# Attention probabilities turned by a product with a diagonal of reciprocal row sums, in a two-layer kernel on one core

## Chip, cores and metric

The kernel runs on one core of one Trainium2 chip. The metric is the device time of one execution in microseconds (us), as the median of several runs. TensorE (PE) does the matrix products, VectorE (DVE), ScalarE (ACT) and GpSimd (POOL) the elementwise work, SyncE (SP) issues the transfers. PEld is the loading of a product's stationary operand, which can run beside a product.

## What is computed

A normalised input goes through causal latent attention and through a routed mixture of 32 experts, and both results are added to the input. Cut to what matters here, for 2 sequences of 1024 tokens and 16 heads:

```python
scores = jnp.einsum('bthd,bshd->bhts', q, k) * scale
scores = jnp.where(causal[None, None], scores, jnp.finfo(scores.dtype).min)
probs = jax.nn.softmax(scores, axis=-1)
out = jnp.einsum('bhts,bshd->bthd', probs, v).reshape(b, t, H * D)
return out @ wo
```

The softmax divides each row of exponentials by its sum. The kernel works with the exponentials and divides later.

## The kernel before

Three stages follow one another. `prepare` normalises the input and makes latents; `attend` does the attention (from about 50 to 731 us of the profiled span); `mix` does the experts.

**Tiling of the attention.** Heads go in 8 pairs (`e` is the head within a pair), each for 2 sequences (`b`), so there are 16 pair steps, numbered `s`. A pair step goes through 8 query tiles `t` of 128 queries. The first tile sees 128 keys, the last 1024. Each engine runs an order written out by hand: `body(i)` lists, per engine, what it does in tile `t` for heads 0 and 1, and semaphores tie the engines together.

**One tile of one head.** PE makes the scores in `ps_s` by `scores` (lines 662 to 664). DVE adds the mask, takes the row maximum and leaves it in `nm` by `maximum` (line 1032). ACT takes exponentials into `prob` and row sums into `lsum` by `exponent` (line 859). PE turns `prob` block by block (128 queries by 128 keys) into `ps_t` by `turn` (line 675), one tile later than the scores. ACT and DVE copy `ps_t` to `pt` by `take_turned` (lines 869 and 1041). PE multiplies the turned blocks with the values by `values` (line 690), two tiles later than the scores, into `ps_o`; the two heads use one half of `ps_o`'s partitions each. A tile `t` has `t + 1` blocks per head, so a pair step has 2 x 36 blocks and the stage has 1152.

**The division.** `ps_o` holds outputs with queries along the free axis, so the reciprocals have to lie along that axis too. After four tiles (a half, `c`) DVE takes the 8 reciprocals per partition by `invert` (line 1048). ACT widens them to 512 columns by `widen` (line 876). PE turns these by `spread` (line 708, the entries `L0` and `Lp` of the hand-written order), ACT takes the result to `rec` (line 882), and DVE multiplies `ps_o` by it into `on` by `normalise` (line 1054). `on` is split into a high and a low part (`out_hi` on ACT, `out_low` on POOL) and goes through `out_products` (lines 719 to 721); DVE adds the result to `yacc` (line 1061).

**Beside this** the order places the projections for the next pair step: PE makes them (line 638), DVE and POOL rotate them (`rope_products` on DVE, lines 997 and 998; lines 1193 and 1195 on POOL), and DVE splits weights in `split_a` (lines 1013 to 1019).

**Kinds of product.** `turn` and `spread` call `nc.tensor.transpose` on float32, with the data as stationary operand and the unit matrix `ident` as moving one. `values` (line 690), the gate and key products in `prepare` (lines 317 and 324), and the folding of weights (line 63) are float32 products by `nc.tensor.matmul`. Line 324 has 8 products for each of 4 chunks, with a stationary operand of 128 columns and 96 moving columns; line 63 has 4 per call, 128 stationary and 64 moving columns; line 317 has 6 per chunk with 512 moving columns. The scores and projections use the float32r format.

Of the kernel before, what the change touches and what calls it, by code (L numbers as in the profile page):

```python
# [33 lines left out]
P = 128  # L34
# [364 lines left out]
STAGE = ["QR0", "Lp", "KR0", "QL0", "QR1", "KR1", "Yp0", "Yp1", "L0", "B", "QL1", "WA", "Y0", "Y1"]  # L399
TURNS = {"QR0": "W0", "KR0": "W1", "QL0": "W2", "QR1": "W3"}  # L400
SPARE = {"Lp": 0, "QR1": 0, "W3": 0, "KR0": 1, "KR1": 1, "W1": 1}


def misc_order(first=False, last=False):
# [3 lines left out]
    for b in range(B):  # L408
        for name in STAGE:
            if (name in ("B", "WA") and b) or (first and b == 0 and name in ("Lp", "Yp0", "Yp1")):  # L410
                continue
# [75 lines left out]
def attend(nc, d, keep):  # L487
    ctx = ExitStack()
    with ctx:
# [11 lines left out]
        rec, on, ohi, olo = tensors(nc, ctx, [  # L501
            ("rec", [P, CH], F32), ("on", [P, CH], F32), ("ohi", [P, CH], F32R), ("olo", [P, CH], F32R)])
# [4 lines left out]
        nm, lsum, linv = tensors(nc, ctx, [("nm", [P, 2], F32), ("lsum", [P, 2, TPC, 2], F32), ("linv", [P, 2, TPC, 2], F32)])  # L507
# [8 lines left out]
        def bank_of(b, name):  # L516

            if b is None:
# [12 lines left out]
        linv_done, widened, rec_copied, on_done, ohi_done, olo_done, y_added = (sem("linv_done"), sem("widened"), sem("rec_copied"), sem("on_done"),  # L531
                                                                       sem("ohi_done"), sem("olo_done"), sem("y_added"))
# [14 lines left out]
        def consumed(i, b, name):  # L547
# [11 lines left out]
            if name in ("L0", "Lp"):  # L559
                return rec_copied, s * 2 + (name == "L0")  # L560
# [35 lines left out]
        def _(pe):  # L596
# [71 lines left out]
            def turn(s, t, e, g):  # L668
# [42 lines left out]
            def reciprocals(i, b, name, s, c):  # L711
                pe.wait_ge(widened, s * 2 + c + 1)
                side(i, b, name, spread)
# [15 lines left out]
            def body(i):  # L729
                for b in range(B):  # L730
# [4 lines left out]
                    def also(name):  # L735
# [10 lines left out]
                        elif name == "Lp":  # L746
                            if earlier:
                                reciprocals(i, b, name, s - 1, 1)
# [10 lines left out]
                    for t in range(TILES):  # L759
# [45 lines left out]
                        else:  # L805
# [4 lines left out]
                            if t < TILES - 1:  # L810
                                also(("L0", "QL1")[t - TPC - 1])
# [763 lines left out]
```

## Time and profile before

| | us |
|---|---|
| median of 3 runs | 1140.23 (1138.33 to 1140.56) |
| the profiled execution | 1139.54 |
| its span, first to last instruction | 1137.8 |
| PE busy in the span | 1109.4 (98%) |
| DVE busy | 733.0 (64%) |
| ACT busy | 635.4 (56%) |
| POOL busy | 487.4 (43%) |
| granted TensorE clock, mean | 0.998 |

The page of the profile lists groups of instructions by line: how many, their summed busy time and the mean of one. PE records overlap: a record shows when a product is in the array, and the next may start before its end. What a product costs is therefore read from the distance between starts in the view in order of time, not from its own duration. A float32 `matmul` of the program appears as two records, each with its own load of the stationary operand.

### The profile page before, as it was taken

To read this page: it belongs to the slowest core of one execution; us is meant where nothing else is said; L and a number is where in the kernel's file an instruction comes from. 1 tells how busy PE (TensorE), PEld (TensorE's weight loads), DVE (VectorE), ACT (ScalarE), POOL (GpSimd) and SP (SyncE) were. 2 spreads that over 40 slices of the span, in tenths; PEclk is the share of its full clock that TensorE was granted. 3 is DMA by queue.
4 is the path that set the end of the run, shared out by engine and by line. 5 is a ranking of instruction groups with operands and counts; after the bars stand their busy time and mean duration, and the time that the engine had idled before them with its cause. 6 is when DMAs were issued, how large, how long until landed. Compare 5 with 4: busy or idle time off the path is not lost. (4 is left out here: it accounts for less than half of the span.)

```text
span 1137.8 us, 23926 instructions
## 1 busy us (share of the span) xinstructions
PE 1109.4 (98%) x8096; PEld 948.7 (83%) x8096; DVE 733.0 (64%) x1540; ACT 635.4 (56%) x1285; POOL 487.4 (43%) x383
## 2 busy tenths in 40 slices
PE   6989999999999999999999999999999999999998
PEld 3668888888888888888888888788888888888887
DVE  6878778678688688687687775564444454444444
ACT  3575766766766766767667767443333333333332
POOL 0265455456456466456456452132333223333232
PEclk9999999999999999999999999999999999999999
DMA  8100000000000000000000021163333334333333
GB/s 295 56 19 19 3 19 20 1 18 18 0 17 19 0 18 18 0 17 19 0 18 0 1 66 31 43 190 115 111 111 115 97 119 145 111 115 97 117 109 101
DMA packets 26343, 67.87 MB, mean 60 GB/s; under 512 B 3061, under 2 KB 9461, under 8 KB 26297
## 3 DMA queue, kind: packets, MB, share of 16 engines
q1 hardware_dynamic: 26152, 67.24, 19.2%
q8 instruction: 23, 0.38, 0.1%
q14 instruction: 24, 0.19, 0.1%
q10 hardware_dynamic: 144, 0.07, 0.0%
HBM read 62.82 MB, written 4.47 MB: 59 GB/s over the span
## 5 line engine op out<-in xcount | busy, mean ns | idle before, releaser
L859 ACT ACTIVATE prob<-ps_s,nm 128x128 f32<-128x128 f32 (+7 forms) x256 | 189.7, 741 | 164.0 <-DVE nm L1032 162.1
L1468 POOL TENSOR_TENSOR qhi<-t,qhi 128x512 fp32r<-128x512 f32 x95 | 122.3, 1288 | 277.7 <-ACT qhi L1406 277.7
L1032 DVE CUSTOM_DVE_ANT_0 ps_s<-ps_s,causal 128x128 f32<-128x128 f32 (+7 forms) x256 | 195.4, 763 | 53.5 <-PE ps_s L664 45.8
L675 PE MATMUL ps_t<-ident,prob 128*128 128x128 f32 x1152 | 177.5, 275 | 3.5 <-ACT pt L869 2.3
L675 PEld LDWEIGHTS ps_t<-ident,prob 128*128 128x128 f32 x1152 | 136.5, 140 | 29.4 <-issue 9.9
L690 PE MATMUL ps_o<-pt,kvn 128*64 128x128 f32 x2304 | 154.0, 278 | 0.1
L690 PEld LDWEIGHTS ps_o<-pt,kvn 128*64 128x64 f32 x2304 | 123.2, 136 | 29.6 <-issue 16.5
L1440 DVE TENSOR_TENSOR t<-t,routing 128x512 f32<-128x512 f32 x64 | 45.0, 703 | 145.2 <-ACT t L1400 140.1
L1041 DVE COPY pt<-ps_t 128x128 f32<-128x128 f32 (+2 forms) x192 | 102.0, 531 | 49.2 <-PE ps_t L675 47.2
L1406 ACT ACTIVATE qhi<-t 128x512 fp32r<-128x512 f32 x95 | 60.1, 633 | 121.0 <-DVE t L1445 121.0
L1400 ACT ACTIVATE t<-ps_s 128x512 f32<-128x512 f32 x94 | 56.2, 598 | 124.6 <-PE ps_s L379 124.6
L869 ACT ACTIVATE pt<-ps_t 128x128 f32<-128x128 f32 (+2 forms) x192 | 97.0, 505 | 27.3 <-PE ps_t L675 24.7
L1214 POOL TENSOR_TENSOR olo<-on,ohi 128x512 fp32r<-128x512 f32 x31 | 39.9, 1287 | 141.9 <-ACT ohi L903 141.9
L1208 POOL TENSOR_TENSOR qlo<-t,qhi 64x512 fp32r<-64x512 f32 x62 | 79.2, 1278 | 48.1 <-ACT qhi L897 39.9
L1193 POOL TENSOR_TENSOR xtf<-xtf,sinv 128x512 f32<-128x512 f32 x62 | 80.0, 1291 | 17.9 <-DVE xtf L998 14.0
L1195 POOL TENSOR_TENSOR t<-t,xtf 128x512 f32<-128x512 f32 x62 | 79.8, 1286 | 4.9
L662 PE MATMUL ps_s<-keys,qhi 128*128 128x384 f32 (+4 forms) x192 | 75.7, 395 | 3.2 <-ACT prob L859 3.2
L662 PE MATMUL ps_s<-khi,qhi 128*128 128x384 f32 (+4 forms) x192 | 74.2, 386 | 0.1
L1335 PE MATMUL ps_y<-keys,qhi 128*128 128x256 f32 x256 | 72.3, 282 | 1.5 <-POOL qhi L1468 1.5
L1337 PE MATMUL ps_y<-keys,qhi 128*128 128x256 f32 x256 | 72.5, 283 | 0.0
L1336 PE MATMUL ps_y<-keys,qhi 128*128 128x256 f32 x256 | 72.4, 283 | 0.0
L1445 DVE TENSOR_TENSOR t<-t,ps_s 128x512 f32<-128x512 f32 x95 | 65.3, 687 | 9.3
(270 smaller groups left out, 2805.3 us busy)
## 6 DMA issues: line engine op xcount, KB each, us to landing
routing<-wT_scratch SPq DMA_DIRECT2D x34, 256.0 KB, 3.7
raw_a<-in_e SPq DMA_DIRECT2D x17, 384.0 KB, 3.0
cosv<-in_e SPq DMA_DIRECT2D x17, 384.0 KB, 3.0
sinv<-wT_scratch SPq DMA_DIRECT2D x17, 384.0 KB, 3.6
raw<-in_e SPq DMA_DIRECT2D x17, 384.0 KB, 3.1
routing<-wT_scratch SPq DMA_DIRECT2D x16, 384.0 KB, 3.3
raw_a<-in_a SPq DMA_DIRECT2D x8, 512.0 KB, 3.3
raw_b<-in_b SPq DMA_DIRECT2D x8, 480.0 KB, 4.0
```

Source lines behind the costliest of these rows:

```text
L662: nc.tensor.matmul(out[:, 0:width], qhi[b][e][:, q], khi[b][e][:, kk], start=True, stop=False, skip_group_check=True)
L675: mm = nc.tensor.transpose(ps_t[x][:, at * P:(at + 1) * P], prob[t % 2][e][:, j * P:(j + 1) * P], ident[:, :])
L690: mm = nc.tensor.matmul(ps_o[64 * e:64 * e + 64, at], kvn[:, b * 8 + j, :], pt[t % 2][:, e, j, :], start=j == 0, stop=j == t)
L859: nc.scalar.activation(prob[t % 2][e][:, 0:len(halves) * width].rearrange("p (h k) -> p h k", k=width), ps_s[e][:, 0:len(halves), 0:width] ...
L869: nc.scalar.activation(pt[t % 2][:, e, blocks[0]:blocks[-1] + 1, :].rearrange("p j q -> p (j q)"), ps_t[0][:, 0:len(blocks) * P], ACT.Copy ...
L1032: nc.vector.tensor_tensor_reduce(out=s_ps, in0=s_ps, in1=bias, scale=-1.0, scalar=-MASKED, op0=ALU.add, op1=ALU.min, accum_out=nm[:, e:e + ...
L1041: nc.vector.tensor_copy(pt[t % 2][:, e, blocks[0]:blocks[-1] + 1, :].rearrange("p j q -> p (j q)"), ps_t[1][:, 0:len(blocks) * P]).then_in ...
L1193: nc.gpsimd.tensor_tensor(sh[:, g, :], sh[:, g, :], sinv[:, c * CH:(c + 1) * CH], ALU.mult).then_inc(rope_sin, 1)
L1195: nc.gpsimd.tensor_tensor(t1[:, g, :], t1[:, g, :], sh[:, g, :], ALU.add).then_inc(rope_sum, 1)
L1208: nc.gpsimd.tensor_tensor(lo[to_b][e][rows, cs], t1[rows, g, :], hi[to_b][e][rows, cs].bitcast(F32), ALU.subtract).then_inc(rope_lo, 1)
L1337: mm = nc.tensor.matmul(to, hl[:, c, tokens], whi[q][:, wide], start=False, stop=True, skip_group_check=True)
L1468: nc.gpsimd.tensor_tensor(hl[:, c, :], hf[:, c, :], hh[:, c, :].bitcast(F32), ALU.subtract).then_inc(h_lo, 1)
```

## The change

The turn becomes a product that also divides. For each head and tile, DVE takes the reciprocals of the 128 row sums (`divide`: a reciprocal of one column, then `ident` times that column into `over`, a 128 x 128 diagonal matrix). `turn` waits for `over` and calls `nc.tensor.matmul` with `prob` as stationary operand and `over` as moving one, instead of `nc.tensor.transpose` with `ident`. The turned block then holds normalised probabilities. `invert`, `widen`, `spread` with `L0` and `Lp`, `take_reciprocals` and `normalise` go; ACT copies `ps_o` to `on` by `take_values` where it took `rec`. `add_out` of `Yp1` moves to a later place in tile 5 of DVE's order.

```diff
-STAGE = ["QR0", "Lp", "KR0", "QL0", "QR1", "KR1", "Yp0", "Yp1", "L0", "B", "QL1", "WA", "Y0", "Y1"]
+STAGE = ["QR0", "KR0", "QL0", "QR1", "KR1", "Yp0", "Yp1", "B", "QL1", "WA", "Y0", "Y1"]
...
-        nm, lsum, linv = tensors(nc, ctx, [("nm", [P, 2], F32), ("lsum", [P, 2, TPC, 2], F32), ("linv", [P, 2, TPC, 2], F32)])
+        nm, lsum, linv = tensors(nc, ctx, [("nm", [P, 2], F32), ("lsum", [P, 2, TPC, 2], F32), ("linv", [P, 2], F32)])
+        over = [[ctx.enter_context(nc.sbuf_tensor(f"over{par}{e}", [P, P], F32)) for e in range(2)] for par in range(2)]
...
-                pe.wait_ge(exp_done, s * U + 2 * t + e + 1)
+                pe.wait_ge(over_done, s * U + 2 * t + e + 1)
                 ge(pe, copied[x], before)
                 for at, j in enumerate(groups_of(t)[g]):
-                    mm = nc.tensor.transpose(ps_t[x][:, at * P:(at + 1) * P], prob[t % 2][e][:, j * P:(j + 1) * P], ident[:, :])
+                    mm = nc.tensor.matmul(ps_t[x][:, at * P:(at + 1) * P], prob[t % 2][e][:, j * P:(j + 1) * P], over[t % 2][e][:, :],
+                                          start=True, stop=True)
...
-            def spread(out):
-
-                for t in range(TPC):
-                    mm = nc.tensor.transpose(out[:, t * P:(t + 1) * P], rec[:, t * P:(t + 1) * P], ident[:, :])
-                return mm
...
-            def widen(s, c):
-
-                act.wait_ge(linv_done, s * 2 + c + 1)
...
-            def take_reciprocals(n, ps):
...
+            def take_values(s, c):
+
+                act.wait_ge(pv_done, 2 * (s * TILES + (c + 1) * TPC))
+                ge(act, olo_done, s * 2 + c)
+                nc.scalar.activation(on[:, :], ps_o[:, :], ACT.Copy).then_inc(on_done, 1)
...
-            def invert(s, c):
...
-            def normalise(s, c):
-                dve.wait_ge(rec_copied, s * 2 + c + 1)
-                dve.wait_ge(pv_done, 2 * (s * TILES + (c + 1) * TPC))
-                ge(dve, olo_done, s * 2 + c)
-                nc.vector.tensor_tensor(on[:, :], ps_o[:, :], rec[:, :], ALU.mult).then_inc(on_done, 1)
+            def divide(s, t, e):
+
+                dve.wait_ge(exp_done, s * U + 2 * t + e + 1)
+                nc.vector.reciprocal(linv[:, e:e + 1], lsum[:, t // TPC, t % TPC, e:e + 1]).then_inc(linv_done, 1)
+                dve.wait_ge(linv_done, s * U + 2 * t + e + 1)
+                nc.vector.tensor_scalar(out=over[t % 2][e][:, :], in0=ident[:, :], scalar1=linv[:, e:e + 1], scalar2=None,
+                                        op0=ALU.mult).then_inc(over_done, 1)
...
+                        if t == TPC:
+                            divide(s, t - 1, 1)
                         maximum(s, t, 0)
+                        if has and t != TPC:
+                            divide(sp, tp, 1)
...
+                            if t == TPC - 1:
+                                divide(s, t, 0)
                             if t > TPC:
                                 take_turned(sp, tp, 1, 1)
                             else:
                                 take_turned(sp, tp, 1, 0)
+                            if t != TPC - 1:
+                                divide(s, t, 0)
                             maximum(s, t, 1)
```

On PE, in tile 1 of a pair step with `b` = 1, this stood in a row before (`ps_o<-pt,kvn` are the values products, `ps_t<-ident,prob` the turns, `ps_s<-ident,rec` the turn of the reciprocals; the moving operand's name comes first):

```order
L662 MATMUL ps_s<-khi,qhi 128x256
L663 MATMUL ps_s<-klo,qhi 128x256
L664 MATMUL ps_s<-khi,qlo 128x256
L690 MATMUL ps_o<-pt,kvn 64x128 x16
L708 MATMUL ps_s<-ident,rec 128x128 x4
L675 MATMUL ps_t<-ident,prob 128x128 x2
L662 MATMUL ps_s<-khi,qhi 128x256
```

And this stands there after the change:

```order
L661 MATMUL ps_s<-khi,qhi 128x256
L662 MATMUL ps_s<-klo,qhi 128x256
L663 MATMUL ps_s<-khi,qlo 128x256
L690 MATMUL ps_o<-pt,kvn 64x128 x16
L674 MATMUL ps_t<-over,prob 128x128 x2
L661 MATMUL ps_s<-khi,qhi 128x256
```

The four turns of the reciprocals are gone, the turns of `prob` have `over` in place of `ident`, and nothing else moved.

On DVE, from the rotation at the start of tile 1 to the maximum of tile 2 (`ISA ps_s,nm<-ps_s,causal` is the maximum, `ISA nm` its read-out, `COPY pt<-ps_t` is `take_turned`, `on<-ps_o,rec` is `normalise`), before:

```order
L997 TENSOR_TENSOR t<-ps_x,cosv 128x512
L998 STREAM_SHUFFLE xtf<-ps_x 128x512
L1032 ISA ps_s,nm<-ps_s,causal 128x256
L1032 ISA nm 128x1
L1041 COPY pt<-ps_t 128x128
L1032 ISA ps_s,nm<-ps_s,causal 128x256
L1032 ISA nm 128x1
L1054 TENSOR_TENSOR on<-ps_o,rec 128x512
L1032 ISA ps_s,nm<-ps_s,causal 128x384
```

And after:

```order
L969 STREAM_SHUFFLE xtf<-ps_x 128x512
L1003 ISA ps_s,nm<-ps_s,causal 128x256
L1003 ISA nm 128x1
L1018 RECIPROCAL linv<-lsum 128x1
L1020 TENSOR_SCALAR over<-ident,linv 128x128
L1012 COPY pt<-ps_t 128x128
L1018 RECIPROCAL linv<-lsum 128x1
L1020 TENSOR_SCALAR over<-ident,linv 128x128
L1003 ISA ps_s,nm<-ps_s,causal 128x256
L1003 ISA nm 128x1
L1003 ISA ps_s,nm<-ps_s,causal 128x384
```

Each tile has two pairs of `RECIPROCAL` and `TENSOR_SCALAR` more, between the maxima; the product of `ps_o` with `rec` has left DVE.

## Rows read from the trace of the kernel before

**Rows 1.** The page, parts 1 and 2: busy time, and PE in 40 slices.

```profile
PE 1109.4 (98%) x8096; PEld 948.7 (83%) x8096; DVE 733.0 (64%) x1540; ACT 635.4 (56%) x1285; POOL 487.4 (43%) x383
...
PE   6989999999999999999999999999999999999998
```

**Rows 2.** Busy time of each engine in a stretch: the attention, 60 to 725 us.

```profile
core 0: us, PE busy (x) PEld busy (x) DVE busy (x) ACT busy (x) POOL busy (x), PEclk, DMA share, GB/s
...
60.00:725.00 665.00, 659.24 (x5563) 562.68 (x5561) 501.23 (x1156) 451.09 (x985) 355.92 (x277) 1.00 0.05 15
```

**Rows 3.** Instructions by line and shape: PE's float32 products; count, busy us, mean ns.

```profile
L675 PE MATMUL ps_t<-ident,prob 128*128 128x128 f32 x1152 | 177.5, 275 | 3.5 <-ACT pt L869 2.3 <-DVE pt L1041 1.2
L690 PE MATMUL ps_o<-pt,kvn 128*64 128x128 f32 x2304 | 154.0, 278 | 0.1
...
L708 PE MATMUL ps_x<-ident,rec 128*128 128x128 f32 x68 | 10.2, 273 | 0.0
...
L708 PE MATMUL ps_s<-ident,rec 128*128 128x128 f32 x60 | 9.8, 287 | 0.0
```

**Rows 4.** PE in order of time, one pair step: start us, length us, instruction, records.

```profile
307.91 1.06 PE L675 MATMUL ps_t<-ident,prob 128*128 128x128 f32 x8
308.73 0.48 PE L638 MATMUL ps_x<-q1hi,rhi 128*128 128x512 f32 x1
309.05 0.40 PE L638 MATMUL ps_x<-q1lo,rhi 128*128 128x512 f32 x1
309.28 0.40 PE L638 MATMUL ps_x<-q,rhi 128*128 128x512 f32 x1
...
310.42 1.97 PE L690 MATMUL ps_o<-pt,kvn 128*64 128x128 f32 x32
312.32 0.66 PE L708 MATMUL ps_s<-ident,rec 128*128 128x128 f32 x4
...
324.36 0.66 PE L675 MATMUL ps_t<-ident,prob 128*128 128x128 f32 x4
```

**Rows 5.** PE in order of time, in the first stage: float32 products, 128-column stationary operands.

```profile
28.02 1.92 PE L324 MATMUL ps_n<-wkg,xT 128*128 128x96 f32 x16
29.79 1.03 PE L63 MATMUL ps_t<-raw_a 128*128 128x64 f32 x8
30.65 5.37 PE L317 MATMUL ps_l<-xT,wl 128*128 128x512 f32 x12
35.86 1.04 PE L307 MATMUL ps_t<-ident,xn 128*128 128x128 f32 x8
```

**Rows 6.** DVE in order of time, in the first stage: small and single-input instructions.

```profile
31.44 0.18 DVE L137 RECIPROCAL rinv<-std 128x4 f32<-128x4 f32 x1 [0.27 <-ACT std L226]
31.66 0.16 DVE L139 TENSOR_TENSOR rtmp<-rinv 128x4 f32<-128x4 f32 x1
...
32.45 1.38 DVE L148 TENSOR_SCALAR xn<-x,mv,rinv 128x256 f32<-128x256 f32 x4
33.75 0.35 DVE L172 CAST rhi<-raw_a 128x384 fp32r<-128x384 f32 x1
```

**Rows 7.** DVE in order of time, tiles 1 to 4 of the same pair step; brackets: idle before.

```profile
310.24 0.69 DVE L997 TENSOR_TENSOR t<-ps_x,cosv 128x512 f32<-128x512 f32 x1 [0.54 <-PE ps_x L638]
...
313.23 0.29 DVE L1041 COPY pt<-ps_t 128x128 f32<-128x128 f32 x1 [1.26 <-PE ps_t L675]
...
313.94 0.69 DVE L1054 TENSOR_TENSOR on<-ps_o,rec 128x512 f32<-128x512 f32 x1
...
316.69 0.42 DVE L1041 COPY pt<-ps_t 128x256 f32<-128x256 f32 x1 [0.28 <-PE ps_t L675]
...
323.53 0.83 DVE L1032 CUSTOM_DVE_ANT_0 ps_s<-ps_s,causal 128x640 f32<-128x640 f32 x1
```

**Rows 8.** One line's instructions on DVE: duration ns min/median/max.

```profile
L1017 DVE CAST rhi<-raw_a x7: 644/1343/1345, 89.1 to 591.9; 128x384 fp32r<-128x384 f32 x7
```

**Rows 9.** POOL in order of time, the same pair step, two of its instructions in a row.

```profile
318.17 1.29 POOL L1193 TENSOR_TENSOR xtf<-xtf,sinv 128x512 f32<-128x512 f32 x1
319.54 1.28 POOL L1195 TENSOR_TENSOR t<-t,xtf 128x512 f32<-128x512 f32 x1
```

More of the change, by code:

```diff
@@ L409, in misc_order @@
         for name in STAGE:
-            if (name in ("B", "WA") and b) or (first and b == 0 and name in ("Lp", "Yp0", "Yp1")):
+            if (name in ("B", "WA") and b) or (first and b == 0 and name in ("Yp0", "Yp1")):
                 continue
@@ L500, in attend @@
         t1 = keep["t1"]
-        rec, on, ohi, olo = tensors(nc, ctx, [
-            ("rec", [P, CH], F32), ("on", [P, CH], F32), ("ohi", [P, CH], F32R), ("olo", [P, CH], F32R)])
+        on, ohi, olo = tensors(nc, ctx, [
+            ("on", [P, CH], F32), ("ohi", [P, CH], F32R), ("olo", [P, CH], F32R)])
         wst = t1[0:E, :, :].rearrange("p g c -> p (g c)")
@@ L745, in also @@
                                 fold_a(i, b, i + 1)
-                        elif name == "Lp":
-                            if earlier:
-                                reciprocals(i, b, name, s - 1, 1)
-                        elif name == "L0":
-                            reciprocals(i, b, name, s, 0)
                         elif name[:2] == "Yp":
@@ L780, in body @@
                             products()
-                            also("Lp")
                             turns(0)
@@ L809, in body @@
                             turn(sp, tp, 0, 1)
-                            if t < TILES - 1:
-                                also(("L0", "QL1")[t - TPC - 1])
+                            if t == TPC + 2:
+                                also("QL1")
                             products()
@@ L841, in _ @@
             pe.wait_ge(olo_done, 2 * s + 2)
+            pe.wait_ge(y_added, s * 4 + 2)
             for m, out in enumerate((ps_x, ps_t[0])):
@@ L930, in body @@
                         if t == 1 and earlier:
-                            take_reciprocals(misc(i, b, "Lp"), bank_of(b, "Lp"))
+                            take_values(s - 1, 1)
                         if has and t == 1:
@@ L946, in body @@
                         exponent(s, t, 1)
-                        if t == 0 and earlier:
-                            widen(s - 1, 1)
                         if more and t in (TPC - 1, TPC):
@@ L980, in _ @@
             silu(0)
+            take_values(s, 1)
             out_hi(s, 1, BEFORE_LAST + len(LAST) - 1)
@@ L1081, in body @@
                             rope_products(i, b, "KR1", s + 1)
-                        if t == TPC + 1 and earlier:
-                            add_out(misc(i, b, "Yp1"), ps_x, s - 1, 1 - b, 1, 1)
                         if t == TPC + 2 and b == 0:
@@ L1087, in body @@
                             split_a(i, b, i + 1)
+                        if t == TPC:
+                            divide(s, t - 1, 1)
                         maximum(s, t, 0)
+                        if has and t != TPC:
+                            divide(sp, tp, 1)
                         if has and (t == 0 or t > TPC):
                             take_turned(sp, tp, 0, 1)
-                        if t == 0 and earlier:
-                            invert(s - 1, 1)
                         if more and t == 2:
@@ L1107, in body @@
                             add_out(misc(i, b, "Y0"), ps_x, s, b, 0, 0)
+                        if t == TPC + 1 and earlier:
+                            add_out(misc(i, b, "Yp1"), ps_x, s - 1, 1 - b, 1, 1)
                         if t == 0:
@@ L1116, in body @@
                                 take_turned(sp, tp, 1, 0)
+                            if t != TPC - 1:
+                                divide(s, t, 0)
                             maximum(s, t, 1)
-                        if t == 1 and earlier:
-                            normalise(s - 1, 1)
                         if t == TILES - 1:
@@ L1166, in _ @@
             n = BEFORE_LAST + len(LAST)
-            invert(s, 1)
+            divide(s, t, 1)
             take_turned(s, t, 0, 1)
             take_turned(s, t, 1, 1)
-            normalise(s, 1)
             gs, hf = keep["gs"], keep["hf"]
```

36 lines of the change are left out of this document (6 added, 30 removed).

## The prediction

> **What bounds the kernel now.** I read the page's busy times first, then the stretches, then PE in order of time. PE is busy 98% of the span and 9 tenths or more in nearly every slice [rows 1]. From 60 to 725 us, the attention, it is busy 659.24 of 665 us at a granted clock of 1.00, which is the 2.4 GHz level; DVE has 501, ACT 451 and POOL 356 us there [rows 2]. So PE is the bound, it has about 5.8 us of idle time to give back, and whatever PE gains or loses in this stage the kernel gains or loses nearly whole. The other engines matter only where PE comes to wait for them. The change touches the turn of the probabilities, 1152 records on PE [rows 3], so its price per block is the main question.
>
> **What a turn costs now.** A turn's record lasts 275 ns, but records overlap, so I go by starts. Eight turns start at 307.91 and the next product at 308.73: 0.82 us. That next product then takes 0.32 us to its successor where its sister takes 0.23 [rows 4], so another 0.09 us is the run's tail: 0.91 / 8 = 0.113 us for each turn. There is one record for each turn: the program has 16 x 72 = 1152 of them, and so has the trace.
>
> **What a product costs in its place.** The new instruction is a plain float32 product, and each of those leaves two records: the program has 1152 values products and the trace 2304 [rows 3]. No row shows one with 128 stationary and 128 moving columns, so I bound it. From below: 32 records of the values products take 310.42 to 312.32, 0.0594 us each [rows 4], 0.119 us a product; but they have 64 stationary columns and the two heads write different halves of the partitions; at 0.0594 against the 0.108 that line 317 will show below for as many moving columns, two of them must be at work together. With 128 stationary columns, the 16 records of line 324 (96 moving columns) take 28.02 to 29.79, 0.111 us each, and the 8 of line 63 (64 moving) 0.86 us, 0.1075 each: the time hardly follows the moving columns, so the load of 128 columns sets it. From above: line 317 with 512 moving columns takes 5.21 us for 12, 0.434 us a record [rows 5]; a quarter of that is 0.1085 for 128 columns, again about the load's time. The two values records that share the array need 2 x 0.0594 = 0.119 us for 128 loaded and 128 moving columns. So a record of the new product should take 0.111 (the load hides the streaming) to 0.119, and a product 0.221 to 0.238. I take 0.230, between the two nearest rows: 0.117 more than the turn. Outer ends: 0.215 (line 63's rate) and 0.242 (0.121 a record, if load and stream disturb each other a little more).
>
> 1152 x 0.117 = **+134.8 us** (bounds +117.5 and +148.6), all on the path, since PE has nothing to hide it under.
>
> A rule of the skill goes further than the row. The Trainium skill (TensorE: Matmul & The Clock Gate, Terms) calls the transpose mode "4× faster for FP32", and its page Perfetto Trace Analysis (Transposes) asks that a logical transpose be a transpose, not a matmul; that speaks against this change. The trace agrees on the direction but has a turn held to 0.113 us, the rate of the loads, so that the gap between the forms should be two here and not four.
>
> **What goes from PE.** Line 708 has 68 + 60 = 128 turns [rows 3] at the same 0.113: **-14.5 us**. They stand in runs of four in PE's stream, so this too is whole.
>
> **What moves on the other engines.** DVE gets 256 times a reciprocal of one column and a scaled copy of 128 columns. The reciprocal of 4 columns starts 0.22 us before its dependent successor; four scaled copies of 256 columns (line 148, with column scalars too) take 32.45 to 33.75, 0.325 each [rows 6]. At about 1 ns for a column (line 148 gives 0.325 us for 256, so at most 1.27 ns) 128 columns fewer leave 0.16 to 0.20, and with the wait between the two I take 0.45 us for a `divide`. That is 115 us more on DVE, less 32 products of 0.69 us (22 us) and 32 reciprocals. DVE's 501 us become about 590 of a stage that is then some 785 us long, so on average it is no more loaded than now. ACT loses a widening per half and exchanges a copy for a copy; both are off the path. The moved addition of `Yp1` only has to come before the fold of the next weights, late in tile 5.
>
> On average is not enough, since the tiles differ. `turn` now waits for `over`, and queued behind it on PE are the next scores. The tight place is tiles 1 to 4, where DVE also has the rotations. From the start of the first rotation at 310.24 to the maximum of tile 4 at 323.53 it takes 13.29 us, of which 1.26 + 0.28 are waits and 0.64 the product that goes [rows 7]: 11.1 us of work. Seven `divide` come in before the turn of head 1 of tile 3: 11.1 + 3.15 = 14.3 us. PE comes to that turn at 324.36 [rows 4], 14.1 us after 310.24; it loses four turns (-0.45) and has 16 blocks at +0.117 before it (+1.9): 15.5 us. DVE has 1.2 us to spare and will still wait now and then, up to the 1.5 us it waits today; so PE stands still for 0 to 0.3 us here. I take 0.2 x 16 pair steps = **+3 us** (0 to 10 with the late tile 7 of `b` = 0, where the weight split delays the maximum).
>
> **Sum.** 1139.5 (the profiled execution: span 1137.8 and 1.7 around it) + 134.8 - 14.5 + 3 = 1262.8. The median of the runs shown is 0.7 above that execution. Forecast: **1263 us**; its own range, from the bounds, 1242 to 1284.
>
> **The rivals.**
> - *DVE becomes the bound in the short tiles.* A single-input copy from and to SBUF took 0.355 us in the first stage [rows 6] but 1.343 in the median beside a working POOL [rows 8], and POOL works in instructions of 1.29 us one behind the other in just these tiles [rows 9]. If the scaling of `ident` is held in the same way, half a POOL instruction on average makes a `divide` 0.65 us longer: DVE needs 14.3 + 4.6 = 18.9 us against PE's 15.5, 3.4 us in each pair step, 54 in all. If only some are held it is 15. That gives 1275 to 1314, with 1295 in the middle. For it: those rows. Against it: line 148, which has the new instruction's form, ran at a one-column-a-nanosecond rate as if through one port, though with POOL idle. The Trainium skill (SBUF — State Buffer, on the two separate sides) says that a VectorE instruction that uses two ports and a GpSimd instruction exclude each other for their whole length. The cast's rows agree with that; whether the new scaling uses two ports no row shows.
> - *Not slower.* If the 128-column product can be kept at the pace of the values product, 0.119 us, because the loads of its two records overlap as two half-wide ones do, then 1152 x 0.006 = +7, and 1139.5 + 7 - 14.5 + 3 = 1135 us, 0.4% faster. The point from which it decides is a product of 0.126 us: below it the 128 turns saved outweigh the rest. Against it: lines 324 and 63, at 0.215 to 0.221.
> - *Four times.* If a product takes the place of four turns, 0.452 us, the sum is 1139.5 + 1152 x 0.339 - 14.5 + 0 = 1515 us. Against it: line 324's two records. It is what the Trainium skill's figure (TensorE: Matmul & The Clock Gate, Terms) would make of it, read literally.
> - *The change doesn't do what it says* (the product lowered to a turn, one record): the time of "not slower", within 2 us.
>
> **How the numbers follow.** The forecast has 0.65, the DVE rival 0.26, not slower (with the last rival) 0.05, four times 0.03, and 0.01 is left for a mishap I don't see. The range holds the forecast's own range but for a sliver and most of the DVE rival: 1243 to 1308. About 0.2% (2.3 us) is what a measurement of this kernel can tell from no change; every case but "not slower" is far above it, and that one is mostly beyond it below: faster 0.04, same 0.01, slower 0.95.
>
> **What would show it.** The turn's line with 2304 records on PE and starts 0.11 to 0.12 us apart confirms the main term; 1152 records or a run of 16 blocks in under 2 us refutes it. The line of the turned reciprocals must be gone. PE should stay at 97% or more busy in the attention with waits of the turn on `over` in the tens of us at most: waits above 30 us in all, and `TENSOR_SCALAR` records of 0.6 us or more, mean the DVE rival. The experts' stage from the end of the attention on must keep its length; if it doesn't, my sum lacks a term.

## The result, and the profile after

The changed kernel takes 1323.63 us in the median (1321.73 to 1328.6), where the kernel before took 1139.86 us beside it: a ratio of 1.1618, 95% interval 1.1589 to 1.1648. That is 183.8 us slower. The forecast was 123 us slower, and its range ended at 1308.

The page of the changed kernel, part 1 and two lines of part 3 (the answer to [rows 1]); the kernel before had 23 packets and 0.38 MB on queue q8, one of the two that bring instructions:

```profile
PE 1247.7 (94%) x9120; PEld 1078.5 (82%) x9120; DVE 876.3 (66%) x1988; ACT 619.8 (47%) x1253; POOL 486.9 (37%) x383
...
q8 instruction: 71, 1.16, 0.4%
```

Two stretches of it, the attention (as [rows 2]) and the experts, columns as there:

```profile
60.00:900.00 840.00, 790.70 (x6517) 686.73 (x6518) 642.47 (x1603) 433.08 (x950) 355.55 (x277) 1.00 0.04 12
920.00:1320.00 400.00, 394.25 (x2270) 347.42 (x2268) 179.35 (x245) 151.40 (x236) 121.66 (x95) 1.00 0.40 119
```

PE is idle for 49.3 of 840 us in the attention, where it was idle for 5.8 of 665. The experts' stage has PE 98.6% busy and kept its length: from the end of the last values product to the end of the span it is 410.7 us before and 410.0 after. All of the loss lies in the attention. The groups by line and shape (count, busy us, mean ns, idle us of the engine just before them and what ended it), as [rows 3]:

```profile
L674 PE MATMUL ps_t<-over,prob 128*128 128x128 f32 x2304 | 321.7, 282 | 42.4 <-DVE over L1020 42.3
L1020 DVE TENSOR_SCALAR over<-ident,linv 128x128 f32<-128x128 f32 x256 | 158.1, 618 | 9.6
L1018 DVE RECIPROCAL linv<-lsum 128x1 f32<-128x1 f32 x256 | 39.7, 155 | 10.1 <-ACT prob L841 7.5
```

The turn has its 2304 records, and line 708's turns of `rec` are gone. The scaling lasts 0.618 us on average. Its single durations (ns, min/median/max), and all of PE's waits from 60 to 910 us (us in total, times, the longest):

```profile
L1020 DVE TENSOR_SCALAR over<-ident,linv x256: 285/290/1877, 57.7 to 902.9; 128x128 f32<-128x128 f32 x128
```

```profile
PE ps_t L674 <- DVE over L1020: 42.1, 73, 2.9
PE ps_s L661 <- issue: 8.0, 5, 1.8
PE ps_s L661 <- DVE xtf L969: 0.2, 1, 0.2
```

So there are two losses that weren't there before: 42 us of waiting for `over`, and 8 us in five stops that no engine causes. Where the scaling is long, GpSimd is at work. A scaling is called held here when its record is long and ends with the record of a GpSimd instruction beside it. VectorE in order of time in tiles 1 to 4 of one pair step (start us, length us), the stretch that answers to [rows 7]:

```profile
384.00 0.98 DVE L1020 TENSOR_SCALAR over<-ident,linv 128x128 f32<-128x128 f32 x1
...
385.95 0.73 DVE L1020 TENSOR_SCALAR over<-ident,linv 128x128 f32<-128x128 f32 x1
...
387.91 0.28 DVE L1020 TENSOR_SCALAR over<-ident,linv 128x128 f32<-128x128 f32 x1
...
395.76 1.37 DVE L1020 TENSOR_SCALAR over<-ident,linv 128x128 f32<-128x128 f32 x1
397.05 0.55 DVE L1012 COPY pt<-ps_t 128x384 f32<-128x384 f32 x1
```

And GpSimd in the same stretch:

```profile
382.27 2.62 POOL L1176 TENSOR_TENSOR keys<-t,keys 64x512 fp32r<-64x512 f32 x2 [9.56 <-ACT keys L873]
385.31 1.29 POOL L1161 TENSOR_TENSOR xtf<-xtf,sinv 128x512 f32<-128x512 f32 x1 [0.42 <-POOL keys L1176]
386.68 1.27 POOL L1163 TENSOR_TENSOR t<-t,xtf 128x512 f32<-128x512 f32 x1
388.62 1.28 POOL L1182 TENSOR_TENSOR olo<-on,ohi 128x512 fp32r<-128x512 f32 x1 [0.67 <-ACT ohi L879]
...
395.75 1.29 POOL L1161 TENSOR_TENSOR xtf<-xtf,sinv 128x512 f32<-128x512 f32 x1 [3.26 <-DVE xtf L969]
```

The scaling of 384.00 ends at 384.98, GpSimd's second record of line 1176 at 384.89. That of 385.95 ends at 386.68, GpSimd's line 1161 at 386.60 (its next instruction starts at 386.68). That of 395.76 started 0.01 us behind GpSimd's and ends at 397.13, GpSimd's at 397.04. That of 387.91 fell into a gap and took 0.28. It is so throughout: of the 256 scalings 124 last over 0.35 us, and each of the 124 ends within 0.12 us of the end of a GpSimd instruction that it overlaps (where two of GpSimd's stand in one row, its middle counts as an end). The other 132 last 0.285 to 0.291 us.

### The profile page after: what moved, and what is told of

Same layout as the page of the kernel before. It is cut to its first block and busy times, and to the rows that moved or that the text cites. A ratio compares the mean times of both kernels' runs of the same rounds, so it can differ in the third digit from the quotient of the medians.

```text
span 1320.7 us, 26299 instructions
## 1 busy us (share of the span) xinstructions
PE 1247.7 (94%) x9120; PEld 1078.5 (82%) x9120; DVE 876.3 (66%) x1988; ACT 619.8 (47%) x1253; POOL 486.9 (37%) x383
## 3 DMA queue, kind: packets, MB, share of 16 engines
q8 instruction: 71, 1.16, 0.4%
## 5 line engine op out<-in xcount | busy, mean ns | idle before, releaser
L674 PE MATMUL ps_t<-over,prob 128*128 128x128 f32 x2304 | 321.7, 282 | 42.4 <-DVE over L1020 42.3
L674 PEld LDWEIGHTS ps_t<-over,prob 128*128 128x128 f32 x2304 | 289.6, 191 | 81.5 <-DVE over L1020 42.0
L1020 DVE TENSOR_SCALAR over<-ident,linv 128x128 f32<-128x128 f32 x256 | 158.1, 618 | 9.6
```

What stands on the lines that cost most here:

```text
L674: mm = nc.tensor.matmul(ps_t[x][:, at * P:(at + 1) * P], prob[t % 2][e][:, j * P:(j + 1) * P], over[t % 2][e][:, :], start=True, stop=True)
L1020: nc.vector.tensor_scalar(out=over[t % 2][e][:, :], in0=ident[:, :], scalar1=linv[:, e:e + 1], scalar2=None, op0=ALU.mult).then_inc(over_d ...
```

## The experiments

Two explanations stood at first. Either the product costs PE what the forecast says, and the rest of the loss is the diagonal, whose scaling GpSimd holds; or the product itself costs something else than forecast. The theories in the expectations below have letters of their own, which change meaning from run to run. All ratios are against the kernel before on the same chip.

### What the product costs PE

**The product without a division** multiplies by `ident` and leaves the division out, so it waits for the exponentials alone:

```diff
-                pe.wait_ge(over_done, s * U + 2 * t + e + 1)
+                pe.wait_ge(exp_done, s * U + 2 * t + e + 1)
...
-                    mm = nc.tensor.matmul(..., over[t % 2][e][:, :],
+                    mm = nc.tensor.matmul(..., ident[:, :],
...
             def divide(s, t, e):
...
+                return
```

> The changed kernel with the unit matrix as moving operand of the turn's product, which again waits only for the exponentials; VectorE's 256 reciprocals and diagonals are gone. The division is left out. Theory A (a product costs 0.241 us, what was lost beyond that is PE waiting for the diagonal): 1139.5 + 1152 x 0.128 = 147.5, less 14.5, and 8 for the stops without a releaser at the loop's end: 1281 us, and no wait on VectorE. Theory B (a product costs 0.230 as forecast, all else comes from VectorE): 1260 us.

Measured: 1261.08 us, 1.1066 (1.1033 to 1.1098). Its turn by line and shape, PE's waits, and two runs of the turn in order of time:

```profile
L674 PE MATMUL ps_t<-ident,prob 128*128 128x128 f32 x2304 | 311.4, 278 | 0.0
```

```profile
PE ps_s L661 <- issue: 7.8, 5, 1.8
```

```profile
318.75 1.16 PE L674 MATMUL ps_t<-ident,prob 128*128 128x128 f32 x8
319.66 0.39 PE L661 MATMUL ps_s<-khi,qhi 128*128 128x320 f32 x1
...
321.86 0.83 PE L674 MATMUL ps_t<-ident,prob 128*128 128x128 f32 x6
```

PE never waits for the turn here, and the stops of 8 us are there already. The 121.5 us above the kernel before are the products, less the reciprocals' turns (-13.6, measured below), plus 7.8: so 127.3 us, or 0.110 for each block beyond the turn's 0.113: **0.224 us a product**. The records agree: eight start 0.91 us before the next instruction, 0.114 each, and over the whole trace starts within runs of 4 to 14 records lie 0.111 us apart. The 1260 us of the expectation's theory B came out in part by luck: the product is 7.5 us cheaper in all than it took, and the stops, which it left out, cost 7.8.

**Half the moving columns** takes the kernel just described and moves 64 columns of `ident` instead of 128, so that half of each block is left out (two products ahead of the stage fill `ps_t` once):

```diff
-                    mm = nc.tensor.matmul(ps_t[x][:, at * P:(at + 1) * P], ..., ident[:, :],
+                    mm = nc.tensor.matmul(ps_t[x][:, at * P:at * P + 64], ..., ident[:, 0:64],
```

> The kernel without the division (e1_product_no_divide, 1261 us) with 64 moving columns for each turn's product instead of 128; half of every turned block is left out. If the load of 128 stationary columns sets the product's 0.224 us, it stays at 0.215 (line 63's rate) or above and the time between 1250 and 1261 us. If the streaming of the moving columns sets it, it falls towards 0.12 us and the time to about 1140 us.

Measured: 1262.99 us, 1.1075 (1.1052 to 1.1099).

```profile
L674 PE MATMUL ps_t<-ident,prob 128*128 128x64 f32 x2304 | 297.7, 272 | 0.0
```

Half the streaming gives nothing back: the time is 2 us above the run with 128 columns, where streaming as the limit would have given 1140 us. What is left is the price of loading 128 stationary columns twice. That is by exclusion, for no run changes the stationary columns alone; the values products, with 64 of them, go at 0.0594 us a record [rows 4], so it isn't a fixed price of any record either.

**One turn of the reciprocals** is the kernel before with one of four turns in `spread`; three quarters of the columns are divided by sums of other rows:

```diff
-                for t in range(TPC):
+                for t in range(1):
                     mm = nc.tensor.transpose(out[:, t * P:(t + 1) * P], rec[:, t * P:(t + 1) * P], ident[:, :])
```

> The kernel before with one turn of the widened reciprocals per half instead of four; its block is copied to all four places, so three quarters of the queries are divided by the wrong sums. 96 turns fewer at 0.113 us: 10.8 us less, 1128.7 us, a ratio of 0.990 to 0.991. If these turns lay in PE's waiting time, no change.

Measured: 1130.16 us against 1140.32, 0.9909 (0.9893 to 0.9926): 10.2 us for 96 turns, so 13.6 for 128, near the 10.8 us expected.

### What the diagonal costs

**The turn with the division unread** keeps `divide` and the wait for `over`, but turns with `ident` by `nc.tensor.transpose`, one record a block; the division doesn't reach the result:

```diff
-                    mm = nc.tensor.matmul(..., over[t % 2][e][:, :],
-                                          start=True, stop=True)
+                    mm = nc.tensor.transpose(..., ident[:, :])
```

> The changed kernel with the turn by nc.tensor.transpose against the unit matrix, still waiting for the diagonal that VectorE makes. The division is left out of the result. Theory A (VectorE with held scalings is too slow for tiles 1 to 4): PE is 1.9 us faster per pair step there than in the changed kernel, so the 42 us of waits grow to 42 + 16 x 1.9 = 72: 1139.5 - 14.5 + 72 = 1197 us. Theory C (the diagonal costs nothing by itself and PE waits only where the longer products disturb the order): 1125 to 1130 us.

Measured: 1227.91 us, 1.0775 (1.0743 to 1.0806), above both. PE's waits:

```profile
PE ps_t L674 <- DVE over L1019: 61.9, 79, 3.1
PE ps_s L661 <- DVE xtf L968: 7.6, 14, 0.6
PE ps_t L674 <- ACT pt L850: 4.4, 14, 0.5
```

Without the dearer product there are no stops on `issue`, and the instruction queue is back at 23 packets: the stops belong to PE's longer program.

The packets' times bear this out. In the kernel before q8 moves nothing from 209.1 to 639.8 us, and each version with one record a block has such a gap. In the changed kernel a packet comes every 3 to 20 us through that stretch, and in each version with two records they keep coming. The loop over pairs has six rounds of two pair steps, so it returns to its start five times, and the five stops lie 107 us apart, one round. So the longer loop has its instructions brought anew in each round. That PE waits for them in the stops is inferred from this.

The diagonal alone, with PE as quick as before, costs 102 us over the 1126 that the kernel before takes without its reciprocals' turns. That is more than in the changed kernel, as is to be expected when a quicker PE waits for the same VectorE. The 72 us of waits in theory A are borne out (61.9 + 7.6 + 4.4); its sum lacks some 30 us by which PE's busy time grew beside them.

**Short rotation on GpSimd** shortens GpSimd's two rotation instructions to 16 of 512 columns and so leaves most of the rotation out:

```diff
-                nc.gpsimd.tensor_tensor(sh[:, g, :], sh[:, g, :], sinv[:, c * CH:(c + 1) * CH], ALU.mult)
+                nc.gpsimd.tensor_tensor(sh[:, g, 0:16], sh[:, g, 0:16], sinv[:, c * CH:c * CH + 16], ALU.mult)
...
-                nc.gpsimd.tensor_tensor(t1[:, g, :], t1[:, g, :], sh[:, g, :], ALU.add)
+                nc.gpsimd.tensor_tensor(t1[:, g, 0:16], t1[:, g, 0:16], sh[:, g, 0:16], ALU.add)
```

> The changed kernel with GpSimd's two rotation instructions (sine product and sum) on 16 columns instead of 512, so that GpSimd is seldom busy in tiles 1 to 4. Most of the rotation is left out. Theory A (a scaling waits while GpSimd works): the scaling's mean falls from 0.618 us to 0.3 to 0.4, PE's waits for the diagonal from 42 to under 12 us, the time to about 1290 us. Theory D (the number of VectorE instructions alone does it, their length by GpSimd's doing matters little): waits stay above 30 us, the time at 1310 or more.

Measured: 1286.79 us, 1.1291 (1.1235 to 1.1347), 36.8 us below the changed kernel.

```profile
L1020 DVE TENSOR_SCALAR over<-ident,linv 128x128 f32<-128x128 f32 x256 | 110.9, 433 | 9.7
```

```profile
PE ps_t L674 <- DVE over L1020: 15.2, 28, 2.9
PE ps_s L661 <- issue: 8.0, 5, 1.9
```

GpSimd's work is what stretches the scaling: with two of its instructions short, 63 scalings are long instead of 124, nearly all beside the instructions that were left long (lines 1176 and 1182 above all), and more than half of the diagonal's cost is gone: 25.7 us are left of 62.5 (both over the product without a division). The time is theory A's, while mean and waits stayed above its signs (0.3 to 0.4 us, 12 us); no run takes the other holders away.

**A constant factor** (the division left out) and **a product of two tensors** (the division complete) change the form of the scaling, in this order:

```diff
-scalar1=linv[:, e:e + 1], scalar2=None
+scalar1=1.0, scalar2=None
...
-                nc.vector.tensor_scalar(out=over[t % 2][e][:, :], in0=ident[:, :], scalar1=linv[:, e:e + 1], scalar2=None,
-                                        op0=ALU.mult).then_inc(over_done, 1)
+                nc.vector.tensor_tensor(over[t % 2][e][:, :], ident[:, :], linv[:, e:e + 1].broadcast_to([P, P]), ALU.mult).then_inc(over_done, 1)
```

> The changed kernel with the constant 1.0 as factor of the diagonal instead of the column of reciprocals. The division is left out of the result. If the held form is the single-input copy from and to the shared memory whatever its factor, the scaling's minimum falls from 0.285 to about 0.22 us, but its mean stays at 0.5 to 0.6 and the time within 10 us of the changed kernel. If reading the column of factors is what is held, no record is far above the minimum and the time is about 1285 us.

> The changed kernel with the diagonal made by a product of two tensors (ident times the reciprocal column, broadcast along the row) instead of a scaling by a column scalar. In the trace of the changed kernel the two-input subtraction of line 990 lasts 557 to 559 ns each time where the one-input cast of line 988 is stretched. Theory A (the scaling is held by POOL because it is a one-input instruction that takes both ports; two-input ones are not): every record 0.27 to 0.30 us, minimum and maximum together, mean below 0.32; waits of the turn on over below 12 us; 1261 + 2 to 10 = 1263 to 1271 us. Theory B (VectorE is simply too full in tiles 1 to 4, or any instruction from SBUF to SBUF is held): mean 0.43 us or more, 1285 us or more.

Measured: 1298.82 us, 1.1397 (1.1342 to 1.1452), and 1302.14 us, 1.1433 (1.1414 to 1.1452). The scaling's durations with the constant, then with two tensors:

```profile
L1020 DVE TENSOR_SCALAR over<-ident x256: 226/227/1827, 57.2 to 879.3; 128x128 f32<-128x128 f32 x128
```

```profile
L1020 DVE TENSOR_TENSOR over<-ident,linv x256: 291/293/1950, 56.9 to 879.8; 128x128 f32<-128x128 f32 x128
```

Both are held, 83 and 81 times, with means of 0.434 and 0.486 us; the constant's time meets neither of its forecasts, and with two tensors it is theory B's. My theory that a two-input instruction escapes rested on one line's steady rows and is wrong: none of the seven records of line 990 in the changed kernel has a GpSimd instruction beside it. With two tensors one sees the same picture as above:

```profile
639.85 1.04 DVE L1020 TENSOR_TENSOR over<-ident,linv 128x128 f32<-128x128 f32 x1
...
642.36 0.29 DVE L1020 TENSOR_TENSOR over<-ident,linv 128x128 f32<-128x128 f32 x1
```

```profile
639.46 1.28 POOL L1160 TENSOR_TENSOR xtf<-xtf,sinv 128x512 f32<-128x512 f32 x1
```

VectorE's instruction ends at 640.89, GpSimd's at 640.74. Instructions of VectorE that read PSUM aren't stretched: the copy of 128x384 from `ps_t` at 397.05 took 0.55 us beside GpSimd's next one, and in the whole attention its median is 0.56 us beside GpSimd (45 copies) and 0.55 alone (35). The two forms are held less often in part because they win where both engines start together. With starts within 0.01 us of each other, the change's scaling lost all 28 times (1.35 to 1.38 us, GpSimd's 1.26 to 1.29); with a constant, and with two tensors, it won all 14 times (0.23 and 0.29 us), and GpSimd's instruction took 1.37 to 1.38 and 1.43 to 1.45. Why the form decides this stays open.

The Trainium skill (SBUF — State Buffer, on the two separate sides) says that a VectorE instruction in a two-port mode, or with two SBUF inputs beside a GpSimd one that reads SBUF, and the GpSimd instruction exclude each other for the whole length of whichever starts first. The rows above agree for all three forms, but that the starts in the records don't settle the ties: of the change's 124 held scalings 15 start up to 0.04 us ahead of GpSimd's instruction. The page would have told me that the product of two tensors is no way out.

### Cheaper products, and another engine for the diagonal

If `prob` and `over` are float32r, the product leaves one record a block, like the turn; with a free diagonal that would be 1125 us. **Float32r with the diagonal as in the change**, and **float32r with the two-tensor scaling**:

```diff
-[P, (TILES - 1 + par) * P], F32))
+[P, (TILES - 1 + par) * P], F32R))
...
-        over = [[ctx.enter_context(nc.sbuf_tensor(f"over{par}{e}", [P, P], F32)) for e in range(2)] for par in range(2)]
+        over = [[ctx.enter_context(nc.sbuf_tensor(f"over{par}{e}", [P, P], F32R)) for e in range(2)] for par in range(2)]
```

> The changed kernel with prob and over declared float32r, so that the product of the turn is one record with one load as the turn was; the diagonal stays on VectorE as in the change. Theory A (VectorE's diagonal is by itself worth some 100 us, whatever PE does): about 1228 us, as the turn with the unread diagonal took, 1215 to 1240, with 1152 records, and waits of the turn on over of 50 to 70 us. Theory P (the price is PE's two records and little else): 1139.5 - 14.5 + a few us of waits, 1125 to 1150.

> Both together: prob and over in float32r (one record for each block) and the diagonal by the two-input product. Theory A: PE's work is that of the kernel before less the 128 turns, 1125 us; in tiles 1 to 4 VectorE needs 11.1 + 7 x 0.48 = 14.5 us against PE's 13.7, so 0.8 to 1.5 us of standstill in each of 16 pair steps: 1138 to 1150 us, about even with the kernel before. Theory B (the scaling's own length hardly matters, only that it stands in VectorE's order): as with the column scalar, 1215 us or more.

Measured: 1241.17 us, 1.0891 (1.0869 to 1.0912), and 1194.82 us, 1.0486 (1.0468 to 1.0503). The turn in each, by line and shape:

```profile
L674 PE MATMUL ps_t<-over,prob 128*128 128x128 f32 x1152 | 183.6, 280 | 76.4 <-DVE over L1020 71.8 <-ACT pt L851 2.9
```

```profile
L674 PE MATMUL ps_t<-over,prob 128*128 128x128 f32 x1152 | 178.1, 276 | 38.1 <-DVE over L1020 32.7 <-ACT pt L851 4.7
```

The product's second record is gone and PE's time with it, some 135 us (127 for the products, 8 for the stops). With the column 82 of them stay gained (1323.63 to 1241.17 us), with two tensors 107 (1302.14 to 1194.82); the rest came back with longer waits for `over` (71.8 for 42.1 us, and 32.7 for 25.0). The first is 13 us slower than the turn with the unread diagonal, just outside theory A's range, and the second lies between its two theories. It is the best complete version of the division on PE here, and 4.9% slower than the kernel before.

**The diagonal on ScalarE** takes the scaling off VectorE; the reciprocal stays there. In the first order ScalarE's diagonal of head 1 stands ahead of the next exponentials of head 0, and that of head 0 behind those of head 1:

```diff
+            def diagonal(s, t, e):
+
+                act.wait_ge(linv_done, s * U + 2 * t + e + 1)
+                nc.scalar.activation(over[t % 2][e][:, :], ident[:, :], ACT.Copy, scale=linv[:, e:e + 1]).then_inc(over_done, 1)
...
+                        if has:
+                            diagonal(sp, tp, 1)
                         exponent(s, t, 0)
...
                         exponent(s, t, 1)
+                        diagonal(s, t, 0)
```

> The changed kernel, whole computation, with the diagonal made by ScalarE (unit matrix times the column of reciprocals) in place of VectorE; the reciprocals stay on VectorE. Theory A (the product with its loop-end stops is 1261 us, the rest of the changed kernel's time is VectorE held by GpSimd): VectorE loses 158 us, PE's waits for the diagonal fall from 42 to under 15 us, and the time to 1262 to 1280 us. Theory E (the chain from the exponentials over a reciprocal to the turn is too long, whoever makes the diagonal): waits stay above 30 us and the time above 1300 us.

> The kernel with the diagonal on ScalarE, and the exponentials and the diagonal kept in the float32r format, in which a product is one record (so the turned probabilities carry that format's rounding). A record of 128 stationary columns in a run costs 0.11 to 0.117 us, like the turn before: 1139.5 + 1152 x (0 to 0.004) - 14.5, and no loop-end stops: 1125 to 1130 us, if ScalarE's diagonal comes in time; PE is then as fast as in e2_turn_with_divide, and if ScalarE's chain holds it up in tiles 1 to 4 by 1 to 2 us per pair step, 1141 to 1162 us.

Measured: 1449.29 us, 1.2709 (1.2683 to 1.2735), with the plain product, and 1344.15 us, 1.1806 (1.1771 to 1.1842), with float32r. The diagonal's durations with the plain product, and PE's wait with float32r:

```profile
L848 ACT ACTIVATE over<-ident,linv x256: 387/392/407, 56.9 to 1023.1; 128x128 f32<-128x128 f32 x128
```

```profile
PE ps_t L674 <- ACT over L848: 134.9, 115, 2.7
```

On ScalarE the instruction is never held, 407 ns at most, and yet PE waits longer for it (125.8 us with the plain product), far outside what theory A and the float32r forecast allowed. So being held isn't all: a diagonal that stands behind other waits of its engine is as bad. Moving both diagonals (head 1's behind the exponentials of head 0, head 0's ahead of those of head 1, but in tile 0) tests that:

```diff
-                        if has:
-                            diagonal(sp, tp, 1)
                         exponent(s, t, 0)
+                        if has:
+                            diagonal(sp, tp, 1)
...
+                        if t > 0:
+                            diagonal(s, t, 0)
                         exponent(s, t, 1)
```

> As the float32r product with the diagonal on ScalarE, but with ScalarE's diagonals at other places of its order: that of head 1 of the tile before stands behind the exponentials of head 0 (it stood ahead of them), that of head 0 ahead of the exponentials of head 1 (it stood behind them). The work on each engine is the same; only the order differs. Theory A (the 1344 us came from the places: a diagonal stood behind exponentials that wait for VectorE and PE): diagonals stay at 0.39 us, waits of the turn on over fall from 134.9 us to below 40, and the time is 1130 to 1175 us, the floor being 1125. Theory C (a diagonal on ScalarE is late wherever it stands, because the reciprocal reaches ScalarE through VectorE's order): 1300 us or more, waits over 100 us.

> The same places on ScalarE with the plain float32 product, two records for each block. Theory A (without VectorE's share the change costs what the product without a division cost, 1261 us): 1261 to 1285 us. Theory C: 1350 us or more, towards the 1449 us of the first order.

Measured: 1235.16 us, 1.0848 (1.0827 to 1.087), with float32r, and 1330.96 us, 1.1681 (1.1658 to 1.1705), with the plain product. The order was worth 109 and 118 us, with the same work on every engine. Of these 56 and 79 us are idle time of PE. The rest is longer busy time in the first order, where the granted clock was lower too: 0.93 of the 2.4 GHz level against 0.98 from 60 to 840 us with float32r, 0.96 against 1.00 from 60 to 900 us with the plain product. Neither theory had it whole, for 80.6 us of waits are left with float32r and 45.6 with the plain product. The last pair puts the division of head 0 ahead of the copies of turned blocks as well, on ScalarE and, with the two-tensor scaling, on VectorE alone (there without the line on `diagonal`):

```diff
+                        diagonal(s, t, 0)
                         if has and (t == 0 or t > TPC):
                             take_turned(sp, tp, 1, 0)
...
+                        divide(s, t, 0)
                         if t == 0:
                             maximum(s, t, 1)
```

> As the float32r product with ScalarE's diagonal in its second order, with the reciprocal and the diagonal of head 0 ahead of the copies of turned blocks on VectorE and on ScalarE (they stood behind them; these copies wait for PE). In the second order the waits of the turn on over were 80.6 us, the longest of them (1.82 us at 366.59) in the long tiles, where diagonal, copy and turn waited for one another in turn. Theory A (only the place costs): waits below 40 us, 1130 to 1180 us. Theory C (the detour of the reciprocal through VectorE to ScalarE costs whatever the place): 1225 us or more, waits as before at 70 us or more.

> The float32r product with the two-input scaling on VectorE (1194.8 us) and with the division of head 0 ahead of VectorE's copies of turned blocks in every tile. Theory A (part of VectorE's share is the place of the division behind copies that wait for PE): 1140 to 1180 us. Theory H (what is left is the holding by POOL and VectorE's full order in tiles 1 to 4, which no place mends): 1188 to 1205 us.

Measured: 1237.17 us, 1.086 (1.0842 to 1.0878), and 1194.92 us, 1.0486 (1.0469 to 1.0504), the times of theories C and H: this place is worth nothing. With ScalarE the worst wait of a pair step reads so, PE first, then ScalarE:

```profile
367.30 1.02 PE L674 MATMUL ps_t<-over,prob 128*128 128x128 f32 x4 [1.79 <-ACT over L848]
```

```profile
364.15 0.62 ACT L877 ACTIVATE qhi<-t 64x512 fp32r<-64x512 f32 x1
364.80 0.63 ACT L878 ACTIVATE qhi<-t 64x512 fp32r<-64x512 f32 x1
365.45 0.60 ACT L856 ACTIVATE pt<-ps_t 128x512 f32<-128x512 f32 x1
366.07 0.79 ACT L841 ACTIVATE prob<-ps_s,nm 128x640 fp32r<-128x640 f32 x1
366.76 0.19 ACT L841 ACTIVATION_READ_ACCUMULATOR prob<-ps_s,nm 128x1 f32 x1
366.86 0.73 ACT L848 ACTIVATE over<-ident,linv 128x128 fp32r<-128x128 f32 x2
```

VectorE's reciprocal for this diagonal was done at 364.70, and the diagonal came at 366.86, 2.16 us later, behind ScalarE's other work. The granted clock of this execution averaged 0.93 of the 2.4 GHz level from 60 to 840 us, and 0.98 in the order before; but three more executions of the same kernel, at 0.98 over their whole span, took 1236.8 to 1237.7 us where this one took 1235.1. So the clock hides no gain of the place. Whether an order exists in which the float32r version reaches its 1125 us wasn't settled.

## Why the prediction was wrong

| term | forecast us | measured us | by |
|---|---|---|---|
| products in place of turns | +134.8 (117.5 to 148.6) | +127 | product without a division |
| turns of reciprocals | -14.5 | -13.6 | one turn of the reciprocals |
| waiting for `over` | +3 (0 to 10) | +62.5 | changed kernel less the product without a division |
| stops of PE's longer program | not in the sum | +8 | waits on `issue` |
| sum | +123 | +184 | |

The measured column adds up by construction, for its first and third rows are differences that leave nothing over; the turns and the stops were measured by themselves.

- **The main term held.** Two records a product, each at the rate of the load, as [rows 5] had it: 0.224 us, near the lower bound's row (0.221) rather than the 0.230 taken. The rule weighed there (the Trainium skill, TensorE: Matmul & The Clock Gate, Terms, transposes four times as fast for FP32) doesn't fit this kernel: 0.224 against 0.113 is a factor of two. "Not slower" and "four times" are both out.
- **The step that failed is the +3 us for VectorE**, and in it the 0.45 us for a `divide`. In tiles 1 to 4 of the pair step shown, the scalings of the seven divisions last 0.85 us on average (0.98, 0.73, 0.28, 0.97, 0.28, 1.37, 1.36); with the reciprocal's 0.155 and a gap of 0.04 a division takes 1.05. Seven are 4.2 us more than the forecast's 3.15, and 14.3 becomes 18.5 us against PE's 15.5: a standstill of 3.0 us where I took 0.2. In the trace VectorE needs 18.7 us there (382.20 to 400.90), and PE's four waits for `over` add up to 2.1 us; the other 16.7 us up to that turn are 1.2 more than the 15.5 forecast for PE. A second term was missing from the sum altogether: the 8 us of stops.
- **Why it was chosen wrongly.** A `divide` that isn't held takes 0.155 + 0.04 + 0.285 = 0.48 us, so the 0.45 was about right for VectorE alone; what it left out was the neighbour. The price came from line 148 with GpSimd idle [rows 6], and the rows of the cast, 0.355 alone and 1.343 beside GpSimd [rows 6, 8], were left to a rival. The instruction runs beside GpSimd [rows 9]; the rows taken there were the nearer ones. The argument against the rival (a column a nanosecond, as if through one port) fails too: line 148 has the form of the new scaling, and that form, 0.285 us when alone, is held 124 times.
- **The rival was right**: its signs came out (42 us of waits, records of 0.618 us), but its price was too small: 54 us was its upper end and 35 its middle, where 62.5 were measured. Of the 62.5 us, 43.9 are idle time of PE (73.0 us in the span against 29.1 in the product without a division) and 18.7 are busy time (1247.7 against 1229.0, at a granted clock of 0.997 in both). The rival counted standstill alone. That the 18.7 us are the overlap lost around each wait is inferred from this difference, not shown by itself.
- **The range** ended at 1308, below the rival's own 1314. Even 1314 would have been short: the forecast's sum with 62.5 for the 3 and 8 for the stops is 1330 us, and 1323 with the product's measured price.
- The claims that VectorE is on average about as loaded as before (in the attention 642.5 of 840 us, 76%, after 75%) and that the experts keep their length held, and helped nothing: the average hid tiles 1 to 4.

## What to carry to other kernels

Read the price of a small VectorE instruction from a row with the same kind of operands beside the same neighbours: one that reads and writes SBUF alone can cost whatever is left of a GpSimd instruction at its side. When a new wait enters the order of the engine that bounds the kernel, cost it in the tightest stretch, with the producing engine's whole queue ahead of it, and add something for busy time that grows beside the waits. A float32 product that took the place of a transpose of 128 x 128 cost twice as much here, with 128 moving columns as with 64.

## What was not expected of the hardware

- PE stood still five times, 1.6 us on average in the changed kernel, for nothing that an engine did. All versions with two records a block have such stops (four or five, 6.0 to 8.4 us in all), and none with one record; the instruction queue's packets go from 23 to 71 with them (0.38 to 1.16 MB). One such stop in the changed kernel, at the first scores of a pair step:

```profile
267.55 0.32 PE L661 MATMUL ps_s<-keys,qhi 128*128 128x128 f32 x1 [1.63 <-issue]
```

- A factor that is a constant instead of a column takes a scaling of 128 columns from 0.285 to 0.226 us.
- The diagonal on ScalarE in two orders, with the same instructions, differed by 109 us (float32r), of which 56 were idle time of PE.
